# Block-wise FFT mixing: H folded before the W transform, and mixing in plain fp32 on blocks of 128 and 64 rows

## The reference

```python
xf = jnp.fft.rfft2(x, axes=(1, 2), norm='ortho')          # 65 frequencies kw along W, 128 along H
xf = xf.reshape(b, h, wf, 8, 96)                          # 8 blocks of 96 channels
o1r = relu(xr @ w1[0] - xi @ w1[1] + b1[0]);  o1i = relu(xi @ w1[0] + xr @ w1[1] + b1[1])
o2r = o1r @ w2[0] - o1i @ w2[1] + b2[0];      o2i = o1i @ w2[0] + o1r @ w2[1] + b2[1]
o2r, o2i = softshrink(o2r, 0.01), softshrink(o2i, 0.01)
out = jnp.fft.irfft2(o2r + 1j * o2i, s=(128, 128), axes=(1, 2), norm='ortho') + x
```

## Time and profile before

| | |
|---|---|
| median of 3 runs | 5806.42 us |
| profiled execution | 5807.0 us, span 5805.2 us |
| mean granted TensorE clock | 0.983 |
| TensorE matmul busy | 5558.5 us, 96% |
| VectorE, ScalarE, GpSimd busy | 71%, 65%, 53% |
| DMA | 414 MB, 70 GB/s over the span |

### The profile page before, as it was taken

One profiled execution on the slowest core, in us unless ns is written; L12 is line 12 of the kernel. 1 busy time (PEld: TensorE's weight loads), 2 busy tenths in 40 slices (PEclk: granted clock), 3 DMA queues, 4 the chain that ended last, 5 costly groups with the idle time before them and its releaser, 6 DMA issues.

```text
span 5805.2 us, 115095 instructions
## 1 busy us (share of the span) xinstructions
PE 5558.5 (96%) x36736; PEld 5058.7 (87%) x36736; DVE 4148.0 (71%) x8579; ACT 3751.7 (65%) x6288; POOL 3055.2 (53%) x2420
## 2 busy tenths in 40 slices
PE   7999999999999999999999999999999999999999
PEld 7888988889888898888988888888889888898888
DVE  5777677676777777777777777677776777767676
ACT  5666666666666666666666666666666666666665
POOL 4445564455644556544555446554465544555445
PEclk9999999999999999999999999999999999999999
DMA  4331233312333213332133331333312333123311
GB/s 92 88 89 45 46 88 88 90 48 42 88 88 90 57 38 84 88 90 64 39 76 88 90 72 37 70 88 90 81 37 60 88 90 88 39 51 88 90 45 44
DMA packets 1070797, 413.95 MB, mean 71 GB/s; under 512 B 1069920, under 2 KB 1070048, under 8 KB 1070176
## 3 DMA queue, kind: packets, MB, share of 16 engines
q1 hardware_dynamic: 1070176, 406.13, 29.8%
HBM read 204.76 MB, written 201.33 MB: 70 GB/s over the span
## 4 chain that ended last, share of the span: by engine, by line
PE 82%; issue 12%; DVE 4%; ACT 1%; POOL 1%; DMA 0%; SPq 0%; DVEq 0%; ACTq 0%; POOLq 0%
PE ps L351 20%; PE ps L372 16%; PE ps L425 11%; PE ps L427 11%; PE ps L389 6%; PE ps L390 6%; PE ps L391 6%; PE ps L445 3%; PE ps L448 3%; DVE x L690 2%; PE ps L387 2%; ACT z_or_packed L485 1%; DVE clamped L673 1%; DVE x L688 1%; DVE ydg L601 0%
## 5 line engine op out<-in xcount | busy, mean ns | idle before, releaser
L351 PE MATMUL ps<-tab,z_or_packed 128*128 128x128 f32 x12288 | 1476.1, 285 | 199.3 <-ACT z_or_packed L485 195.1
L351 PEld LDWEIGHTS ps<-tab,z_or_packed 128*128 128x128 f32 x12288 | 1459.0, 200 | 237.7 <-ACT z_or_packed L485 228.6
L752 POOL TENSOR_TENSOR x<-x,vcopy 128x480 f32<-128x480 f32 (+1 forms) x416 | 602.3, 1458 | 1193.4 <-ACT vcopy L583 1191.2
L734 POOL TENSOR_TENSOR z_or_packed<-z_or_packed 96x384 f32<-96x384 f32 (+1 forms) x704 | 696.1, 989 | 971.5 <-DVE z_or_packed L632 583.2
L743 POOL TENSOR_TENSOR zlo<-z_or_packed,zhi 96x768 fp32r<-96x768 f32 x608 | 1107.3, 1821 | 84.8 <-ACT zhi L513 83.8
L673 DVE TENSOR_SCALAR clamped<-ps 128x576 f32<-128x576 f32 (+2 forms) x736 | 530.8, 721 | 755.8 <-PE ps L427 755.8
L372 PE MATMUL ps<-tab,ydg 128*96 128x130 f32 x8192 | 1018.9, 274 | 17.8 <-DVE ydg L601 17.8
L425 PE MATMUL ps<-w2r,hid 97*128 97x192 f32 x4160 | 1019.0, 325 | 0.0
L427 PE MATMUL ps<-w2i,hid 96*128 96x192 f32 x4160 | 1015.1, 325 | 0.0
L372 PEld LDWEIGHTS ps<-tab,ydg 128*96 128x96 f32 x8192 | 971.9, 163 | 30.7 <-ACT ydg L494 23.0
L601 DVE COPY ydg<-ps 128x512 f32<-128x512 f32 (+2 forms) x832 | 549.0, 660 | 542.0 <-PE ps L351 536.2
(11 more groups left out here) (49 smaller groups left out, 7179.3 us busy)
## 6 DMA issues: line engine op xcount, KB each, us to landing
x<-in_x SPq DMA_DIRECT2D x128, 1536.0 KB, 14.9
out<-x SPq DMA_DIRECT2D x352, 480.0 KB, 5.6
out<-x SPq DMA_DIRECT2D x32, 432.0 KB, 4.6
out<-x SPq DMA_DIRECT2D x32, 240.0 KB, 4.3
out<-x SPq DMA_DIRECT2D x32, 192.0 KB, 3.8
w2r<-in_w SPq DMA_DIRECT2D x16, 72.0 KB
w1g<-in_w SPq DMA_DIRECT2D x16, 36.0 KB
w1i<-in_w SPq DMA_DIRECT2D x16, 36.0 KB
```

Of the source, the lines that this page charges most:

```text
L351: mm = pe.matmul(ps[:, bank, j * 128:(j + 1) * 128], packed_slot(stage, g)[:, j, :], rhs, start=True, stop=True)
L734: pool.tensor_tensor(zz[:, 0, 0:n, :], zz[:, 2, 0:n, :], zz[:, 1, 0:n, :], ALU.add).then_inc(zsum_ready, 1)
L752: pool.tensor_tensor(xp, xp, vcopy[g % 3][:, 0:b - a, :], ALU.add).then_inc(plus_ready, 1)
```

## The change

The forward lines are folded along H: `fold` adds row h and row 128 - h (64 columns) and subtracts them (63 columns), so that the two transforms along W give results whose H transform is real. They are two matmuls per channel, one on output partitions 0-63, one on 64-126. Row 0 goes apart. The H transform is then one product of 128 rows of spectrum with a 128 x 128 table, and gives real and imaginary channels (192) stacked: the first 128 of them (`zbig`) and the last 64 (`zsmall`, two kw side by side on the partitions). Both mixings multiply this stack by real 192 x 192 matrices, cut at 128; `mixing_layout` lays them out on the host. F32R, the split and the three-product form are gone. The groups have 4 kw; there are 17, the last with one. The bias of the second layer is added by VectorE.

```diff
-RING = 4
+RING_A = 6
+RING_H = 6
+def packer_a(g):
+    return "pool" if g % 3 == 0 or g < RING_A else "dve"
+def mover(stage, g):
+    if stage == 0:
+        return "dve" if g % 4 == 3 else "act"
+    return "dve" if g % 2 else "act"
+GROUP_PAIRS = ([[(3, 4), (5, 6)], [(0, 64), (1, 2)]]
+               + [[(k, k + 1), (k + 2, k + 3)] for k in range(7, 63, 4)] + [[(63, None)]])
+EDGES = 1
...
+        def fold(engine, p, g):
+            engine.tensor_tensor(slot[:, :, 0:HALF], rows(1, HALF + 1), rows(H - 1, HALF - 1, -1), ALU.add)
+            return engine.tensor_tensor(slot[:, :, HALF:127], rows(1, HALF), rows(H - 1, HALF, -1), ALU.subtract)
...
-                            mm = pe.matmul(ps[:, bank, j * 128:(j + 1) * 128], packed_slot(stage, g)[:, j, :], rhs, ...)
+                    pe.wait_ge(y_ready, NF * q + NF - 3)
+                    pe.matmul(ps[:, ROW0_BANK, 0:CB], mat("fwd_w"), xs[p][:, 0, :], ...).then_inc(row0_done, 1)
...
+                            pe.matmul(o[0:HALF], slot[:, 0:HALF], mat("fwd_w"), start=True, stop=True)
+                            mm = pe.matmul(o[HALF:127], slot[:, HALF:127], mat("fwd_w_odd"), start=True, stop=True)
...
+                def fwd_big(q, u):
+                    if u:
+                        pe.wait_ge(zbig_ready, NU * q + u)
+                    for k, kw in enumerate(evens(u) + odds(u)):
+                        mm = pe.matmul(ps[:, ZBIG_BANK, k * H:(k + 1) * H], <rows of kw>[:, 0:BIG], mat("fwd_h"), ...)
+                def fwd_small(q, u):
+                    for k, pair in enumerate(GROUP_PAIRS[u]):
+                        for i, kw in enumerate(pair):
+                                mm = pe.matmul(ps[i * SMALL:(i + 1) * SMALL, ZSMALL_BANK, k * H:(k + 1) * H],
+                                               t[:, s + 1, CUT:CB], mat("fwd_h"), start=True, stop=True)
+                def mix1_whole(q, u):
+                    pe.wait_ge(zbig_ready, NU * q + u + 1)
+                    pe.wait_ge(zsmall_ready, NU * q + u + 1)
+                    if u:
+                        pe.wait_ge(hid_ready, NU * q + u)
+                    for i, a, b in halves:
+                        pe.matmul(ps[:, BIG_BANK + i, 0:n], mix_part("w1_big")[:, 0:BIG], zbig[u % 2][:, a:b], ...)
+                    pe.matmul(ps[0:r, SMALL_BANK, 0:n], mix_part("w1_small_small")[0:r, 0:r], zsmall[u % 2][0:r, 0:n], ...)
+                def mix1_columns(q, u):
+                    for i, a, b in halves:
+                        mm = pe.matmul(ps[i * SMALL:(i + 1) * SMALL, SMALL_BANK, 0:n],
+                                       mix_part("w1_big")[:, BIG:2 * CB], zbig[u % 2][:, a:b], ...)
+                def mix1_rows(q, u):
+                    for i, a, b in halves:
+                        half = slice(i * SMALL, (i + 1) * SMALL)
+                        mm = pe.matmul(ps[:, BIG_BANK + i, 0:n], mix_part("w1_small_big")[half], zsmall[u % 2][half, 0:n], ...)
+                def mix2_rows(q, u):
+                            mm = pe.matmul(ps[:, OUT_BANK + i, ...], hsmall[u % 2][half, k * H:(k + 1) * H],
+                                           mix_part("w2_small")[half], start=False, stop=True, ...)
+                    mm.then_inc(mix2_done, 1)
+                def mix2_whole(q, u):
+                    pe.wait_ge(hid_ready, NU * q + u + 1)
+                    if u:
+                        pe.wait_ge(bias_done, NU * q + u)
+                    for k in range(n + len(odds(u))):
+                        pe.matmul(o, hbig[u % 2][:, k * H:(k + 1) * H], mix_part("w2_big"), ...)
...
+                        for it in range(NU + 2):
+                            if it < NU: fwd_big(q, it)
+                            if it >= 2: mix2_whole(q, it - 2)
+                            if 1 <= it < NU + 1: mix1_whole(q, it - 1)
+                            if it < NU: fwd_small(q, it)
+                            if 1 <= it < NU + 1: mix1_columns(q, it - 1)
+                                                 mix1_rows(q, it - 1)
+                            if it >= 2: mix2_rows(q, it - 2)
+                            if it == EDGES + 4: merge(q)
...
+                def shrink(q, u):
+                    dve.wait_ge(mix2_done, NU * q + u + 1)
+                    dve.tensor_tensor(parts(v), d, b2, ALU.add).then_inc(bias_done, 1)
+                    dve.tensor_scalar(c, v, LAMBD, -LAMBD, ALU.min, ALU.max).then_inc(clamp_done, 1)
+                    dve.tensor_tensor(dst, parts(v)[:, :, first:ne, :], parts(c)[:, :, first:ne, :], ALU.subtract)
...
+                        # GpSimd, a pass:
+                        for g in range(RING_A, NG):
+                            if packer_a(g) == "pool": fold(pool, p, g).then_inc(folded_pool, 1)
+                        if not (last and p == PAIRS - 1):
+                            pool.wait_ge(x_loaded[1 - p], (t + 1 + p) * 16 * LOADS)
+                            pool.wait_ge(line_done, lines_before(q, 1, 0))
+                            fold_first(1 - p)
```

More of the change, by code:

```diff
@@ L74 @@
 TABLE = _at
+FWD = 2 * W
+MIX = {}
+_at = 0
+for _name, _n in (("w1_big", 2 * CB), ("w2_big", 2 * CB), ("w1_small_big", BIG), ("w2_small", 2 * CB),
+                  ("w1_small_small", 2 * SMALL), ("b1", 2), ("b2", 2 * CB)):
+    MIX[_name] = (_at, _at + _n)
+    _at += _n
+MIXED = _at
 def transform_table():
@@ L116, in transform_table, with mixing_layout, part, build @@
     merge_odd = (eye - flip) / 2
-    return np.concatenate([fwd_w / 128, fwd_h, inv_h, inv_even / 128, inv_odd / 128,
+    return np.concatenate([fwd_w / 128, fwd_w_odd / 128, fwd_h, inv_h, inv_even / 128, inv_odd / 128,
                            merge_even, merge_odd], 1).astype(np.float32)
-def build(nc, x, w1, b1, w2, b2, table, out):
+def mixing_layout(w1, b1, w2, b2):
+    import numpy as np
+    w1, b1, w2, b2 = (np.asarray(a, dtype=np.float32) for a in (w1, b1, w2, b2))
+    out = np.zeros((NB, 128, MIXED), np.float32)
+    def part(name):
+        a, b = MIX[name]
+        return out[:, :, a:b]
+    for name, w in (("w1_big", w1), ("w2_big", w2)):
+        o = part(name)
+        o[:, 0:CB, 0:CB], o[:, 0:CB, CB:] = w[0], w[1]
+        o[:, CB:, 0:CB], o[:, CB:, CB:] = w[1][:, 0:CUT], w[0][:, 0:CUT]
+    for lo in (0, SMALL):
+        rows = slice(lo, lo + SMALL)
+        o = part("w1_small_big")
+        o[:, rows, 0:CB], o[:, rows, CB:] = w1[1][:, CUT:], w1[0][:, CUT:, 0:CUT]
+        o = part("w2_small")
+        o[:, rows, 0:CB], o[:, rows, CB:] = w2[1][:, CUT:], w2[0][:, CUT:]
+        part("w1_small_small")[:, rows, rows] = w1[0][:, CUT:, CUT:]
+        part("b1")[:, rows, 1] = b1[1][:, CUT:]
+    part("b1")[:, 0:CB, 0], part("b1")[:, CB:, 0] = b1[0], b1[1][:, 0:CUT]
+    part("b2")[:] = np.concatenate([b2[0], b2[1]], 1)[:, None, :]
+    return out
+def build(nc, x, mix, table, out):
     with ExitStack() as ctx:
@@ L135, in build @@
         ydg = sb("ydg", [128, 128, CB])
[L138 to L158, removed]
@@ L227, in split_count, with mix_part @@
[L227 to L244, removed]
-        def line_bank(stage, g):
-            return (g + 2) % 8 if stage == 0 else g % 8
+        def mix_part(name):
+            a, b = MIX[name]
+            return wts[:, a:b]
@@ L250, in line_moves @@
         def line_moves(stage, g):
             c, n = LINE_GROUPS[g]
[L253 to L259, removed]
+            rows = 127 if stage == 0 else 128
+            return (ydg[0:rows, :, c:c + n],
+                    ps[0:rows, line_bank(stage, g), 0:n * 128].rearrange("p (c k) -> p k c", c=n))
@@ L296, in load_weights @@
[L296 to L316, removed]
-                                sp.wait_ge(y_ready, NF * q + NF + g + 1)
-                                sp.dma_start(dst[:, a:e, :], xs[p][:, a:e, :]).then_inc(stored[p], 16)
-                                lo, hi = H - min(e, H // 2) + 1, H - max(a, 1) + 1
-                                sp.dma_start(dst[:, lo:hi, :], xs[p][:, lo:hi, :]).then_inc(stored[p], 16)
-                                a = e
-                            sp.wait_ge(stored[p], (t + 1) * 16 * STORES)
[L325 to L329, removed]
-                    step(STEPS - 1, True)
@@ L332, in _, with forward_lines @@
+                with sp.Fori(0, STEPS - 1) as t:
+                    step(t, False)
+                step(STEPS - 1, True)
             @block.tensor
             def _(pe):
-                def lines(q, p, stage):
-                    rhs = mat("fwd_w") if stage == 0 else mat("inv_h")
+                def forward_lines(q, p):
+                    pe.wait_ge(y_ready, NF * q + NF - 3)
+                    pe.matmul(ps[:, ROW0_BANK, 0:CB], mat("fwd_w"), xs[p][:, 0, :],
+                              start=True, stop=True).then_inc(row0_done, 1)
@@ new lines, in mix2_rows @@
+                def mix2_rows(q, u):
+                    for k, pair in enumerate(GROUP_PAIRS[u]):
+                        for i in range(2 if pair[1] is not None else 1):
```

(20 more changed lines are left out.)

658 lines of the change are left out of this document (330 added, 328 removed).

## The result

Slower by 3.4%: a median of 6004.08 us (6000.02 to 6005.27, 4 runs) against 5807.22 (5803.06 to 5810.91, 4 runs), ratio 1.0338 [1.0322, 1.0355]. The forecast was 5732, the range 5500 to 6150. The profiled execution took 6003.43 us.

What follows compares the result with a forecast made beforehand. TensorE, 96% busy, was taken to bound the kernel. Streaming 160.7 us plus waits 17.3 made 178.0 a pass; 32 passes, 5696, plus 29, 5 and 1.8 outside the span gave 5732 us, range 5500 to 6150.

Steps and rivals of the forecast that it cites:

- Other engines: Forward lines: VectorE busy 14 of 21.4 us, ScalarE 12, GpSimd folds 1.4 to 1.7 against 2.7 between turns; none binds.
- a helper binds in the forward lines: Rival, chance 0.07: GpSimd's or VectorE's forward-line folds take twice the price, 5 us a pass, total 5890 us.
- Halves beside each other: Forward lines and mixing: half-array matmuls on different halves overlap, costing 60.6 us a pass instead of 106.8.
- n + 1 distances: Half-array products: with starts in program order, n matmuls take n + 1 start distances; forward lines 21.4 us.
- starts aren't bound to program order: Rival, chance 0.15: half-array products run at full rate on both halves, 6.4 us less a pass, total 5527 us.
- Shape changes: Mixing: three changes of array shape in each of 16 rounds, taken at 0 us each, 0.27 kept as upper bound.
- the first rival: Rival, chance 0.27: shape changes in the mixing empty the array, 0.163 or 0.27 us each, total say 5950 us.
- 5.6 to 5.8 us: Sign of the main case: length of a mixing round, with one gap ahead of the whole second products.
- over 6 us: Sign that the forecast is wrong: a mixing round longer than 6 us.
- Bias wait: Mixing: the second mixing's whole products wait for the previous group's bias addition, 0.37 us, 15 times, +5.6 us a pass.
- Start gap: Start of a pass: TensorE's idle falls from 5.75 to about 3 us (even), 0.82 to 0 (odd), -1.8 a pass.
- End of mixing: Last two rounds lack `fwd_big` as cover, +0.9 us; before the inverse lines 1.4 more than now; +2.3 a pass.

Runs made afterwards that it cites:

- e3: Changed kernel with folds walking row by row, channels innermost (strided writes): 5802.65 us, 0.9993 of the kernel before.
- f1: Changed kernel with the edits of e3 and e4 together: 5662.11 us, 0.9753 of the kernel before.
- f4: f1 with each forward-line group's products for rows 0-63 first, then those for 64-126: 5705.0 us, 0.9827 of the kernel before.
- e4: Changed kernel with the first mixing's whole products moved ahead of the second's: 5859.76 us, 1.0098 of the kernel before.

## Why the prediction was wrong

**The step that failed** is "Other engines": "None binds". It put a fold pass of VectorE at 0.376 us, from a copy of 256, and GpSimd's fold of two passes at 1.4 to 1.7 us. Both prices were too low, for two reasons that multiply. First, a fold pass is longer than a copy of as many elements: VectorE's alone is 0.65 to 0.69 us, GpSimd's 1.05. (How much of that is the second operand and how much the stride, no run parts; the order of elements alone moves it as told below.) Second, the two engines slow each other. VectorE and then GpSimd, of the changed kernel, in order of time:

```profile
3019.81 0.66 DVE L285 TENSOR_TENSOR ring_a<-x 128x252 f32<-128x252 f32 x1
3020.39 1.54 DVE L284 TENSOR_TENSOR ring_a<-x 128x256 f32<-128x256 f32 x1
3021.85 1.53 DVE L285 TENSOR_TENSOR ring_a<-x 128x252 f32<-128x252 f32 x1
...
3030.10 0.65 DVE L285 TENSOR_TENSOR ring_a<-x 128x252 f32<-128x252 f32 x1
3030.65 0.68 DVE L284 TENSOR_TENSOR ring_a<-x 128x256 f32<-128x256 f32 x1
```
```profile
3021.37 1.49 POOL L285 TENSOR_TENSOR ring_a<-x 128x252 f32<-128x252 f32 x1
3022.83 1.49 POOL L284 TENSOR_TENSOR ring_a<-x 128x256 f32<-128x256 f32 x1
...
3027.12 1.44 POOL L285 TENSOR_TENSOR ring_a<-x 128x252 f32<-128x252 f32 x1
3032.80 1.19 POOL L284 TENSOR_TENSOR ring_a<-x 128x256 f32<-128x256 f32 x1 [4.24 <-PE ps L381]
...
3046.86 1.05 POOL L285 TENSOR_TENSOR ring_a<-x 128x252 f32<-128x252 f32 x1
3047.87 1.06 POOL L284 TENSOR_TENSOR ring_a<-x 128x256 f32<-128x256 f32 x1
```

While GpSimd stands idle (3028.6 to 3032.8) VectorE's passes start 0.56 us apart (3029.55 to 3032.34, five steps); while VectorE doesn't fold (from 3046.86) GpSimd's start 1.01 apart. Together both start every 1.46 us, near the sum of 1.57: they all but take turns. The Trainium skill, "SBUF — State Buffer", section "SBUF: two separate sides", says that a VectorE instruction with two SBUF inputs and a GpSimd instruction that reads SBUF lock each other out: whichever starts first holds the shared port for its whole length. The trace agrees in kind, with those numbers, and VectorE's copies out of PSUM (0.68, L623) between them were not lengthened. An estimate from these distances: by turns the stage's folds need 26 x 0.56 + 14 x 1.01 = 28.7 us, some 2 less as the last groups are small, and 1.8 us pass before the first fold (3014.25 to 3016.03). That fills most of the 30.2 measured.

Of the miss of 272 us the forward lines, 30.2 against 23.9, are 6.3 x 32 = 202. The mixing adds 2.2 x 32 = 70 (below), the inverse lines 13; the rows give 19 back, and the program's start and end the rest.

e3's order works on both prices: alone, VectorE's passes then start 0.46 us apart and GpSimd's 0.69 (both in f1's trace), so the same sum is 21.6, about TensorE's own length. The rival "a helper binds in the forward lines" was the right one, but I gave it 0.07 and 5 us a pass, and looked at each engine by itself. Taken like that, even the right prices don't bind: 26 x 0.56 + 6 moves x 0.6 = 18.2 us for VectorE and 14.1 for GpSimd, both under 21.4.

**The range** held the 6004 us by luck: its upper part was there for shape changes, at up to 6008 us, and the loss came from elsewhere.

**Halves beside each other: right, and better than "n + 1 distances".** From the lines of an odd pass:

```profile
3200.36 0.27 PE L380 MATMUL ps<-tab,ring_a 128*64 128x128 f32 x1
3200.37 0.27 PE L381 MATMUL ps<-tab,ring_a 128*63 128x128 f32 x1
3200.47 0.27 PE L380 MATMUL ps<-tab,ring_a 128*64 128x128 f32 x1
3200.48 0.27 PE L381 MATMUL ps<-tab,ring_a 128*63 128x128 f32 x1
```

A pair starts every 0.11 us, its two instructions 0.01 apart here and 0.03 in the median of the trace. A product's first instructions on both halves start ahead of its second on either, so this is the rival "starts aren't bound to program order", as f4 shows as well.

**Shape changes: the term 0 was wrong; the first rival's mechanism is real,** at 0.16 to 0.20 us a change. One round of the changed kernel, in the view of the earlier trace rows:

```profile
2920.22 1.16 PE L409 MATMUL ps<-tab,ydg 128*128 128x128 f32 x8
2921.44 1.54 PE L473 MATMUL ps<-wts,hbig 128*128 128x192 f32 x8
2922.81 1.03 PE L436 MATMUL ps<-zbig,wts 128*128 128x256 f32 x4
2923.68 0.59 PE L439 MATMUL ps<-zsmall,wts 128*128 128x256 f32 x2
2924.20 0.66 PE L421 MATMUL ps<-tab,ydg 128*64 128x128 f32 x8
...
2926.50 1.16 PE L409 MATMUL ps<-tab,ydg 128*128 128x128 f32 x8
```

The round is 6.28 us where my sum had 5.89 + 0.37 = 6.26: full halves gave 0.44 back, the three changes took some 0.55, and the bias wait adds 0.30 to that. The sum came out because two errors cancel, which is luck. (The "5.6 to 5.8 us" that I gave for the round, and "over 6 us" as a sign of being wrong, do not fit my own sum.)

**Bias wait: right.** From the start of the last row product (2919.96) to the next whole second products (2921.44) it is 1.48 us, for my 1.42. The 1.06 of cover was too little by the shape change ahead of `fwd_big`: the same stretch without the wait is 1.25 in f1 (2936.33 to 2937.58). So this change hides under the wait, as I wrote, and shows only once the wait is gone. e4, where the wait is covered, gained 144 us, 0.28 a round and not 0.37.

**Start gap: right in kind, better in size.** Idle ahead of an even pass fell from 5.75 to 1.93 us in the passes shown (forecast "about 3"; 1.5 to 2.9 over all passes), ahead of an odd one to nothing.

**End of mixing: too small.** Ahead of the inverse lines 2.99 us of idle stand against 1.89 in the earlier trace rows, 1.1 more where I had 1.4. But the last three whole second products wait 0.73, 1.15 and 1.16 us for VectorE's bias additions, 3.04 together, where I had 0.9 + 3 x 0.37 = 2.0 at most. This 1 us is part of the mixing's 2.2; the rest of it is not traced to a term.

**Open:** in f1 the forward lines still take 24.0, not 21.5. In its even passes some 12 pairs behind the start gap lie 0.21 us apart and not 0.11 (the 1.2 GHz level), 1.2 us; in its odd passes none does. There, gaps of up to 0.9 us, most of them ended by VectorE's folds, make 1.8 us. So the folds still bind a little; no run takes either share alone. Why turns save some 7% against the sum isn't settled either.

## What to carry to other kernels

Where VectorE and GpSimd both work ahead of TensorE on instructions with two operands in SBUF, as these folds do, price them as one stream: add up both engines' instructions, each by its distance alone, and compare that sum with the stage. Take their price from a row with as many operands and the same element order, not from a copy. Putting the short contiguous axis innermost was worth 201 us here. Half-array fp32 products ran two at once at full rate, but each change of array shape cost about 0.16 us, so gather the products of a shape.

## What the hardware showed unasked

- GpSimd and VectorE folds in the same stretch each start every 1.46 us; alone 1.01 and 0.56. Turns are not always fair: in 23 of GpSimd's 832 passes of the changed kernel it took over 3 us. In the one below (GpSimd first) VectorE's passes went by unlengthened, and GpSimd was through 1.07 us after VectorE turned to a copy out of PSUM:

```profile
601.80 4.31 POOL L284 TENSOR_TENSOR ring_a<-x 128x256 f32<-128x256 f32 x1 [4.07 <-PE ps L381]
```
```profile
602.15 0.70 DVE L285 TENSOR_TENSOR ring_a<-x 128x252 f32<-128x252 f32 x1
...
604.46 0.73 DVE L285 TENSOR_TENSOR ring_a<-x 128x252 f32<-128x252 f32 x1
605.04 0.75 DVE L623 COPY ydg<-ps 127x512 f32<-127x512 f32 x1
605.64 0.97 DVE L284 TENSOR_TENSOR ring_a<-x 128x256 f32<-128x256 f32 x1
```

- Two half-array fp32 matmuls start 0.01 to 0.03 us apart, and TensorE finds the second even behind three instructions of the other half (f4; that order costs 0.05 us a group, 43 us in all). The Trainium skill, "TensorE: Matmul & The Clock Gate", part 3, has matmuls start strictly in program order; the trace of f4 does not agree across halves, and the trace decides.
